# Attention layer with experts: PSUM banks for the two score passes, four and two in place of three and three

## The reference

```
c      = layernorm(xh @ Wdkv) * g + b          # latent keys, 128 wide
scores = q_lat @ c.T / sqrt(128), causal mask
w      = softmax(scores)
oh     = (w @ (c @ Wuv)) @ Wo_h                # per head
out    = concat(oh) @ Wo.T + bo
experts: mean over the two experts of the gate's top 2 of relu(xn @ expert_w + expert_b)
```

## Time and profile before

| | |
|---|---|
| median of 3 runs | 1737.25 us (1737.16 to 1741.39) |
| the profiled execution's own time | 1736.69 us |
| its span, first to last instruction | 1734.9 us |
| busy in the span | PE 88%, PEld 49%, DVE 67%, ACT 52%, POOL 33% |
| attention, 264.4 to 1413 us | PE 1036.7 busy of 1148.6, DVE 805.6, ACT 689.9 |
| granted TensorE clock, same stretch | 0.99 |

### The profile page before, as it was taken

One profiled execution on the slowest core, in us unless ns is written; L12 is line 12 of the kernel. 1 busy time (PEld: TensorE's weight loads), 2 busy tenths in 40 slices (PEclk: granted clock), 3 DMA queues, 4 the chain that ended last, 5 costly groups with the idle time before them and its releaser, 6 DMA issues.

```text
span 1734.9 us, 45239 instructions
## 1 busy us (share of the span) xinstructions
PE 1531.7 (88%) x12544; PEld 845.8 (49%) x12545; DVE 1157.8 (67%) x2501; ACT 896.8 (52%) x1628; POOL 579.6 (33%) x780
## 2 busy tenths in 40 slices
PE   4788859899899999999999999999999959999996
PEld 2677845444444444444444444444445425555443
DVE  4777777677777777777777777777777614444467
ACT  1656635565656656665656566665666623333200
POOL 1333312776222222223222222222222333333276
PEclk8999978999999999999999999999999979999998
DMA  5467760232222222232223222232223145555499
GB/s 163 150 207 239 216 177 17 61 91 63 63 62 74 78 64 63 59 90 65 61 61 84 68 65 62 66 87 62 64 59 93 41 157 177 174 171 174 135 362 344
DMA packets 165707, 198.15 MB, mean 114 GB/s; under 512 B 50144, under 2 KB 99296, under 8 KB 165248
## 3 DMA queue, kind: packets, MB, share of 16 engines
q1 hardware_dynamic: 146880, 157.10, 30.8%
q0 software_dynamic: 12992, 35.77, 6.8%
q10 hardware_dynamic: 5760, 4.49, 0.8%
HBM read 108.99 MB, written 62.98 MB: 99 GB/s over the span
## 4 chain that ended last, share of the span: by engine, by line
PE 39%; SPq 25%; issue 11%; DVE 9%; DMA 7%; POOL 4%; ACT 3%; ACTq 0%; DVEq 0%; POOLq 0%
PE PS L1205 12%; PE PS L1258 12%; PE PS L1301 11%; SPq L428 7%; SPq L421 4%; POOL w_hi L688 4%; SPq L443 3%; DVE pm L1017 3%; SPq L441 3%; SPq L440 3%; DMA arena<-mxT 3%; DMA arena<-in_x 2%; PE PS L1283 2%; DVE bv_bc L1038 1%; ACT arena L787 1%
## 5 line engine op out<-in xcount | busy, mean ns | idle before, releaser
L1017 DVE TENSOR_REDUCE pm<-PS 128x1 f32<-128x512 f32 (+3 forms) x1280 | 716.0, 602 | 243.8 <-PE PS L1205 238.1
L1205 PE MATMUL PS<-arena 97*64 97x512 f16 (+7 forms) x5120 | 732.0, 354 | 110.0 <-DVE pm L1017 39.2
L787 ACT ACTIVATE arena<-PS 128x512 f32<-128x512 f32 (+1 forms) x1152 | 603.7, 574 | 356.1 <-PE PS L1205 355.0
L1258 PE MATMUL PS<-arena 128*33 128x512 f32 (+3 forms) x2560 | 655.4, 532 | 0.0
L1205 PEld LDWEIGHTS PS<-arena 96*64 96x64 f16 (+1 forms) x5120 | 355.8, 110 | 490.9 <-issue 189.2
L605 POOL TENSOR_SCALAR_AFFINE_SELECT arena<-arena 128x256 f32<-128x256 f32 (+1 forms) x256 | 110.8, 433 | 637.2 <-ACT arena L787 636.3
L1258 PEld LDWEIGHTS PS<-arena 128*33 128x33 f32 x2560 | 169.5, 111 | 82.5 <-issue 0.7
L1301 PE MATMUL PS<-w_hi,arena 128*128 x576 | 172.7, 382 | 0.8 <-issue 0.8
L1205 PE MATMUL PS<-later,deny 128*64 128x128 f16 x1024 | 166.2, 222 | 0.0
L804 ACT ACTIVATE arena<-PS 128x1024 f16<-128x1024 f32 x72 | 73.7, 1024 | 152.4 <-PE PS L1283 152.4
L1068 DVE SCALAR_TENSOR_TENSOR arena<-PS,eb_bc 128x512 f32<-128x512 f32 x72 | 49.8, 691 | 130.3 <-PE PS L1301 127.9
(11 more groups left out here) (172 smaller groups left out, 1311.9 us busy)
## 6 DMA issues: line engine op xcount, KB each, us to landing
expert_rows<-arena SPq DMA_DIRECT2D x72, 256.0 KB, 2.1
comb_hl<-arena SPq DMA_DIRECT2D x256, 64.0 KB
arena<-q_pieces SPq DMA_DIRECT2D x96, 128.0 KB
arena<-k_pieces SPq DMA_DIRECT2D x96, 128.0 KB
v_rows<-arena SPq DMA_DIRECT2D x8, 1056.0 KB, 6.6
arena<-v_rows SPq DMA_DIRECT2D x32, 264.0 KB
arena<-in_x SPq DMA_DIRECT2D x8, 1024.0 KB, 7.3
xn_rows<-arena SPq DMA_DIRECT2D x16, 512.0 KB, 6.1
```

The source lines that it names most:

```text
L787: a.activation(probs[kk % 4][:, a_ * CH:a_ * CH + w], PS[:, s2_bank(k, x), 0:w], ACT.Exp, scale=SCALE).then_inc(s["exp_done"], 1)
L1017: v.reduce_max(pm[:, c, r, p:p + 1], PS[:, S1_BANK[n], 0:w], AX).then_inc(s["s1_done"], 1)
L1205: last = t.matmul(PS[h:h + P // 2, bank, cols], lhsT[:, h:h + P // 2], rhs, start=start, stop=stop)
L1258: last = t.matmul(PS[rows_, 6 + c % 2, CH - wds[a]:CH], v_sb[pu % 2][:, j + a, :], probs[pk % 4][:, a * off:a * off + wds[a]], start=p_ in ...
```

## The change

The second pass gets two banks (4 and 5), the first pass four (0 to 3). No instruction is added, taken away or moved on any engine; what changes is the bank that an instruction names, and the count that a wait waits for. A piece now waits for the maximum four pieces back, in every place of the head (40 is a multiple of 4), and product x of the second pass for exp x - 2.

```
-        S2_RING, S1_RING = 3, 3
+        S2_RING, S1_RING = 2, 4
         assert NX % S2_RING == 0
...
-            return 3 + (EXPS_TO[k] - len(parts(k)) + x) % S2_RING
+            return S1_RING + (EXPS_TO[k] - len(parts(k)) + x) % S2_RING
...
-        S1_BANK = [n % S1_RING for n in range(NP_ - 1)] + [1]
+        assert NP_ % S1_RING == 0
+        S1_BANK = [n % S1_RING for n in range(NP_)]
         S1_BACK = [min(d for d in range(1, NP_) if S1_BANK[n - d] == S1_BANK[n]) for n in range(NP_)]
```

## The result

| | before | after |
|---|---|---|
| median | 1737.25 us (7 runs, 1732.40 to 1741.39) | 1753.31 us (7 runs, 1745.95 to 1759.74) |
| profiled execution | 1736.69 us | 1750.79 us |
| its span | 1734.9 us | 1749.0 us |

The ratio is 1.0091 with a 95% interval of 1.0063 to 1.0119: the change costs 11 to 21 us. 1752 was forecast, and slower with a chance of 0.75.

The account below looks back on a forecast made before the run. SP's DMA issuing up to unit 12 was taken to bound each round, with PE after it. First pass 0, second pass 0.49 us x 30 heads plus 0.5 made 15.2 us: 1752 us, range 1745 to 1762, widened to 1743 to 1764.

Parts of the forecast that it names:

- SP's round closes over unit 12 and nothing before unit 12 counts: Each 35.42 us round: SP's queue and landing take 19.3 us up to unit 12; other engines' waits there cost nothing.
- Four first-pass banks: 0: First pass: stalls for maxima go, piece 27's of 0.39 to 0.99 us the largest; worth 0 on the chain.
- Two second-pass banks: 0.47 at product 15b, 0.02 at unit 13: Second pass: 15b waits for exp 14b, 0.47 us later; 13b for exp 12b, 0.02 late; 0.49 us per head.
- The share of unit 13: Product 13b, put at 717.03, would need exp 12b, over at 717.01, plus 0.04: 0.02 us late per head.
- The sum: 30 heads x 0.49 = 14.7 us, plus 0.5 for the last head: 15.2 us on 1736.69, giving 1751.9.
- the faster rival: DVE's maxima bound the kernel and the fourth bank pays, at piece 27: 1716 to 1749 us, middle 1732; chance 0.11.
- The clock: Rival: TensorE's clock falls at unit 15 in each head, 51 us with the 15, about 1803; much slower, chance 0.05.
- The milder form: Longer waits at units 8 and 12, a few past 2 us, bring clock falls: up to 8 us more.
- The rule on repeated bubbles: Skill's reading of a repeating bubble on the engine that should be full: too little PSUM; taken as the faster rival.
- taking piece 15's stall away alone moves nothing: Unit 15: four banks remove piece 15's 0.68 us stall, but product 15b behind it still needs exp 14a.

Follow-up runs that it names:

- e1: Changed kernel with the fourth first-pass bank taken back (three and two, one bank unused): 1756.15 us, 1.0103 of the kernel before.
- e5: Kernel before plus three DRAM-to-DRAM DMAs per head in SP's queue at unit 5, inside its closed part: 1835.91 us, 1.0547.
- e6: Kernel before plus three DRAM-to-DRAM DMAs per head at unit 18 of SP's order, where SP sleeps: 1734.96 us, 0.9989.
- e3: Changed kernel (four and two banks) with ACT's rounding of the head's output moved to unit 15: 1697.92 us, 0.9774 of the kernel before.
- e9: Three first-pass and two second-pass banks (one unused), ACT's rounding at unit 15: 1724.73 us, 0.9932 of the kernel before.
- e2: Kernel before (three and three banks) with ACT's rounding moved from ahead of unit 14's exps to ahead of unit 15's: 1721.88 us, 0.9912.
- e7: Kernel before (three and three) with chunk 3's row of maxima first in SP's order at unit 8: 1715.61 us, 0.9859.
- e8: Four and two banks, ACT's rounding at unit 15, chunk 3's row of maxima first in SP's order: 1675.54 us, 0.9628 of the kernel before.
- e4: Changed kernel (four and two) with the rounding one unit later still, ahead of unit 16's exps: 1717.49 us, 0.9879 of the kernel before.

## Why the prediction was right

*SP's round closes over unit 12 and nothing before unit 12 counts.* Right, and shown three ways: 19.28 us from SP's start to unit 12 in both kernels; the fourth bank without worth in e1 (equal rounds); DMAs that cost in e5 and are free in e6.

*Four first-pass banks: 0.* Right. PE's 36.8 us of waits for maxima went, and its wait for the values grew from 13.6 to 30.8 us, about 0.6 us per head, where "up to about 1 us" was said. That of chunk 3's maxima hardly changed, 1.2 us each (32.3 over 27), was 1.1 (28.8 over 26).

*Two second-pass banks: 0.47 at product 15b, 0.02 at unit 13.* Right in place and size: 7.14 us after unit 12 instead of 6.66 is 0.48, the round is 0.50 longer in head 12, 0.47 in the mean of 25 rounds, and PE waits for an exp 30 times, 1.6 us each (47.3 over 30), where 1.3 to 1.6 was said. The share of unit 13 is too small to be shown by itself.

*The sum.* 15.2 us against 14.1 in the profiled executions and 16.1 in the medians. 14.0 of the 14.1 lie between the first and the last head's multiply, 11.8 of them in 25 rounds; how the rest falls on the first and last heads I did not take apart. That the median came within 1.3 us of the forecast is closer than its interval (11 to 21 us) can tell: what carries the prediction is the size of the round, not this nearness. One of its side sums is wrong: with 12 us of relief the faster rival gives 1752 - 12 = 1740, not 1749, so its range was 1716 to 1740. No term of the forecast hangs on it.

*The clock.* The repeated fall at unit 15 did not come: 1.53 us of stall, and no fall behind it. The milder form came once ahead of the last head, at unit 8 of head 28, where the lengthened wait for the values reached 2.04 us:

```profile
1284.88 0.47 PE L1206 MATMUL PS<-arena 97*64 97x512 f16 x4 [2.04 <-DMA arena<-v_rows]
```

```profile
1285.70:1289.00 3.30, 3.30 (x18) 1.36 (x16) 1.57 (x5) 1.57 (x4) 0.00 (x0) 0.50 0.23 47
```

*The rule on repeated bubbles* (the Trainium skill, Perfetto Trace Analysis, "Optimization Strategy"), named in the prediction beside the faster rival, says that they can mean too little PSUM. More PSUM for the first pass removed the bubble here and won nothing (e1), yet it won 27 us in e3 against e9: the bubble at piece 15 was too few banks, hidden behind a late exp. The forecast said that taking piece 15's stall away alone moves nothing, and stopped there; it did not say that the two stalls are one pair, worth 0.4 to 0.5 us per head if only the exp's goes (e2) and 1.2 to 1.3 if both do (e3: the round is 1.21 shorter, and 0.9774 is 39 us below the kernel before). That was the larger finding.

## What to carry to other kernels

Before a wait is priced, find what closes the round. Here it was SP, which slept once per round (3.7 us) and then worked without a pause up to what it feeds: waits of other engines in that stretch cost nothing as long as it stays the longest way round (in e7 and e8, once it was shortened, one of them took over). Two waits that end close to each other on one engine (here 0.64 us apart, piece 15 at 721.50 and product 15b at 722.14) have to be taken away together: banks alone lost 16 us, the order of ACT's work alone won 15, both won 39. When a step is moved, look at every engine that it takes along, and at what stands ahead of it there: one unit more turned 39 us into 21 (e4).

## What the hardware showed that was not expected

The length of a stall does not tell by itself whether TensorE's clock falls to 1.2 GHz behind it. In the kernel before, a stall of 2.01 us was followed by 1.00 and one of 2.13 by 0.53. In the changed kernel 2.04 us was followed by 0.50 (above), and this one, the longest of its attention stage, was followed by 1.00:

```profile
331.21 0.89 PE L1206 MATMUL PS<-arena 97*64 97x512 f16 x6 [3.18 <-ACT arena L788]
```

```profile
331.00:334.50 3.50, 3.29 (x26) 1.32 (x28) 2.03 (x5) 2.79 (x6) 2.94 (x3) 1.00 0.18 40
```

The Trainium skill (TensorE: Matmul & The Clock Gate, "What's actually happening") says that activity is judged in a window that runs free of the program, so that the moment at which the clock changes varies. The traces agree so far that nearly equal stalls (2.01 and 2.04 us) differ in what follows; no run here shows the window.

Three DMAs from DRAM to DRAM of 128 KB each took 1.81 us of SP's issuing (e5), three loads of the same size from DRAM to SBUF 1.30 (L421 in the kernel before, L422 after).
